# The next image's x asked for in 16 pieces, at the pace of the weight slots

## The reference

```python
g = gn(x)                                # 32 groups of 16 channels
h = relu(bn1(conv1x1(g, conv1_w)))       # 512 -> 128 channels
q = bnq(conv1x1(h, q_w))                 # 4 heads x 16
k = softmax(conv1x1(h, k_w))             # 16
v = bnv(conv1x1(h, v_w))                 # 32
content = einsum(k, v)
pos = conv2d(v, emb)                     # 15 x 15, 16 kernels, for every channel of v
h = q . content + q . pos                # 4 heads x 32 = 128 channels
h = bn3(conv1x1(relu(bn2(h)), conv3_w))  # 128 -> 512
out = x + relu(h + g)
```

## Time and profile before

| | us |
|---|---|
| median of 3 runs (lowest, highest) | 5223.51 (5220.97, 5228.06) |
| the profiled execution | 5228.72 |
| its span in the trace | 5227.0 |
| TensorE busy | 4672.8 |
| VectorE busy | 2957.6 |
| ScalarE busy | 2282.6 |
| mean granted TensorE clock | 0.926 |

### The profile page before, as it was taken

One profiled execution on the slowest core, in us unless ns is written; L12 is line 12 of the kernel. 1 busy time (PEld: TensorE's weight loads), 2 busy tenths in 40 slices (PEclk: granted clock), 3 DMA queues, 4 the chain that ended last, 5 costly groups with the idle time before them and its releaser, 6 DMA issues.

```text
span 5227.0 us, 121426 instructions
## 1 busy us (share of the span) xinstructions
PE 4672.8 (89%) x49366; PEld 2740.0 (52%) x49366; DVE 2957.6 (57%) x4695; ACT 2282.6 (44%) x2816; POOL 748.4 (14%) x433
## 2 busy tenths in 40 slices
PE   4899999899999899999899999999988999999897
PEld 2555555555455555555555555455555555555454
DVE  4465565565555565545656556556556555556553
ACT  1444444444444454444444444444444444445443
POOL 0011110111111111101111111111111111011111
PEclk8898999999999999999989998999999899989998
DMA  3678766678666787666786667876667876678765
GB/s 97 190 237 280 239 212 233 232 251 282 216 213 232 239 271 257 196 227 233 250 278 206 218 229 238 281 243 210 243 225 251 281 233 200 236 234 266 262 192 201
DMA packets 540244, 1217.09 MB, mean 233 GB/s; under 512 B 54312, under 2 KB 236588, under 8 KB 539820
## 3 DMA queue, kind: packets, MB, share of 16 engines
q1 hardware_dynamic: 474348, 950.15, 56.1%
q10 hardware_dynamic: 65472, 260.05, 14.0%
HBM read 777.68 MB, written 365.22 MB: 219 GB/s over the span
## 4 chain that ended last, share of the span: by engine, by line
PE 50%; issue 12%; DVE 12%; DMA 8%; SPq 7%; ACT 7%; POOL 2%; ACTq 0%; DVEq 0%; POOLq 0%
PE ring L498 13%; PE ring L643 13%; PE ring L517 9%; PE ring L573 6%; SPq L387 5%; DMA h<-S 4%; PE ring L597 4%; DMA X<-x_dram 3%; PE ring L524 2%; POOL X L1166 2%; ACT region L782 2%; PE ring L607 2%; DVE S L1010 2%; DVE ring L1014 2%; DVE region L965 2%
## 5 line engine op out<-in xcount | busy, mean ns | idle before, releaser
L691 ACT COPY region<-ring 126x1024 f32<-126x1024 f32 x1184 | 1163.2, 1015 | 1137.4 <-PE ring L498 1127.9
L573 PE MATMUL ring<-h,w3T 128*128 128x512 f32 x2048 | 1016.3, 637 | 130.7 <-DVE S L1010 82.1
L517 PE MATMUL ring<-X,w1e 128*128 128x512 f32 x2048 | 911.0, 598 | 49.7 <-DVE w1e L887 28.9
L498 PE MATMUL ring<-Qt,Ep 96*126 96x256 bf16 x5120 | 851.4, 308 | 101.3 <-ACT region L691 65.7
L643 PE MATMUL ring<-region,V 126*32 126x128 f32 x24576 | 875.2, 287 | 20.4 <-issue 20.4
L498 PEld LDWEIGHTS ring<-Qt,Ep 96*126 96x126 bf16 x5120 | 626.6, 152 | 346.9 <-issue 171.2
L643 PEld LDWEIGHTS ring<-region,V 126*32 126x32 f32 x24576 | 675.0, 115 | 240.6 <-issue 230.1
L691 DVE COPY region<-ring 126x1024 f32<-126x1024 f32 x352 | 430.1, 1222 | 630.7 <-PE ring L498 630.7
L863 DVE BATCH_NORM_STATS2 st<-X 128x6 f32<-128x512 f32 x1024 | 624.6, 677 | 207.2 <-DMA X<-x_dram 207.1
L573 PEld LDWEIGHTS ring<-h,w3T 128*128 128x128 f32 x2048 | 381.2, 199 | 570.2 <-issue 366.9
L517 PEld LDWEIGHTS ring<-X,w1e 128*128 128x128 f32 x2048 | 382.4, 190 | 527.9 <-issue 478.2
(11 more groups left out here) (127 smaller groups left out, 3069.5 us busy)
## 6 DMA issues: line engine op xcount, KB each, us to landing
X<-x_dram SPq DMA_DIRECT2D x132, 2048.0 KB, 21.0
out_dram<-X SPq DMA_DIRECT2D x512, 512.0 KB, 9.9
X<-x_dram ACTq DMA_DIRECT2D x124, 2048.0 KB, 9.4
Qt<-q_parts SPq DMA_DIRECT2D x768, 128.0 KB, 4.1
V<-v_windows SPq DMA_DIRECT2D x96, 1024.0 KB, 8.2
h<-S SPq DMA_DIRECT2D x1024, 64.0 KB, 2.0
q_parts<-region SPq DMA_DIRECT2D x128, 256.0 KB, 3.2
v_windows<-region SPq DMA_DIRECT2D x64, 512.0 KB, 5.8
```

Source lines behind the costliest of these rows:

```text
L498: last = nc.tensor.matmul(dst[0:TROWS, i * 256:(i + 1) * 256], taps(u, xo, yo), Q[:, :, xo * BLK + yo, :], start=(i % 2 == 0), stop=True, ...
L517: last = nc.tensor.matmul(dst[:, hh * HALF:(hh + 1) * HALF], w1e[:, c, :], X[:, j, c, hh * HALF:(hh + 1) * HALF], start=(c == 0), stop=(c ...
L573: last = nc.tensor.matmul(dst[:, yb * HALF:(yb + 1) * HALF], w3T[:, t, :], src, start=True, stop=True)
L691: return engine_copy(dst, src)
```

## The change

Three things are changed, and nothing in what is computed.

1. x of the next image is loaded in 16 pieces of 512 KB, one for each chunk j and channel tile c, each with a semaphore of its own. Piece n is issued after `X_AFTER[n]` slots of units 1 and on have been generated by TensorE (24 for the last one, the end of unit 3's slots); the first piece of a chunk still waits for the stores of the chunk too.
2. `load_v3` is issued behind piece 7 instead of behind all of x.
3. The statistics go piece by piece, two parts for each, and stand at other places among VectorE's slots (`STATS_AT`); `c0` waits for the 16 semaphores.

`x_turn` is only counted up, and nothing waits for it.

```diff
@@ -41,7 +41,11 @@
 ACT_SLOTS = [(u, s) for u in range(UNITS) for s in range(NS) if s not in BY_DVE[u]]
 DVE_SLOTS = [(u, s) for u in range(UNITS) for s in range(NS) if s in BY_DVE[u]]
 
-STATS_AT = {0: (0, 0, 0, 0, 0, 1, 1, 1), 1: (1, 1, 1, 2, 1, 1, 2, 1), 2: (1, 1, 1, 2, 1, 1, 2, 1), 3: (1, 1, 1, 1, 1, 2, 1, 1)}
+STATS_AT = {0: (0, 0, 0, 0, 2, 0, 2, 0), 1: (2, 0, 2, 0, 2, 0, 2, 0), 2: (2, 0, 2, 0, 2, 0, 2, 0), 3: (2, 0, 2, 0, 2, 2, 2, 2)}
+
+
+X_AFTER = [0, 1, 2, 4, 6, 7, 9, 11, 12, 14, 16, 18, 19, 21, 23, 24]
+V3_AFTER = 7
 
 
 VEC_TILES = [0, 2, 3, 5, 7, 8, 10, 12, 13, 15]
@@ -265,8 +269,9 @@
         pool_out = sem("pool_out")
         dve_link = sem("dve_link")
 
-        x_in = [sem(f"x_in{j}") for j in range(NCH)]
+        x_in = [[sem(f"x_in{j}{c}") for c in range(CT)] for j in range(NCH)]
         res_in = [sem(f"res_in{j}") for j in range(NCH)]
+        x_turn = sem("x_turn")
         out_done = [sem(f"out_done{j}") for j in range(NCH)]
         q_out = [sem(f"q_out{j}") for j in range(NCH)]
         q_in = [sem(f"q_in{j}") for j in range(NCH)]
@@ -337,8 +342,8 @@
 
         @block.sync
         def _(sp):
-            def load_x(im, j):
-                sp.dma_start(X[:, j, :, :], xv[im, :, :, j * CHUNK:(j + 1) * CHUNK]).then_inc(x_in[j], 16)
+            def load_x(im, j, c):
+                sp.dma_start(X[:, j, c, :], xv[im, :, c, j * CHUNK:(j + 1) * CHUNK]).then_inc(x_in[j][c], 16)
 
             def reload(b, j):
                 sp.dma_start(X[:, j, :, :], xv[b, :, :, j * CHUNK:(j + 1) * CHUNK]).then_inc(res_in[j], 16)
@@ -396,7 +401,8 @@
 
             for j in range(NCH):
                 sp.sem_inc(out_done[j], HEAD)
-                load_x(0, j)
+                for c in range(CT):
+                    load_x(0, j, c)
             sp.dma_start(w1r, w1).then_inc(setup_in, 16)
             sp.dma_start(w3r, w3.rearrange("(t p) c -> p t c", p=P)).then_inc(setup_in, 16)
             sp.dma_start(wqr, wq).then_inc(setup_in, 16)
@@ -437,8 +443,17 @@
                 if not last:
                     for j in range(NCH):
                         sp.wait_ge(out_done[j], b * (16 * CT) + HEAD)
-                        load_x(b + 1, j)
-                load_v3(b)
+                        sp.sem_inc(x_turn, 1)
+                        for c in range(CT):
+                            n = j * CT + c
+                            if n:
+                                sp.wait_ge(w_full, b * (UNITS * NS) + NS + X_AFTER[n])
+                                sp.sem_inc(x_turn, 1)
+                            load_x(b + 1, j, c)
+                            if n == V3_AFTER:
+                                load_v3(b)
+                else:
+                    load_v3(b)
                 shuffle(b, 0)
                 shuffle(b, 1)
 
@@ -557,7 +572,8 @@
                 elif name == "c0":
                     pe.wait_ge(w1e_ready, im + 1)
                     for i in range(NCH):
-                        pe.wait_ge(x_in[i], im * 16 + 16)
+                        for c in range(CT):
+                            pe.wait_ge(x_in[i][c], im * 16 + 16)
                 elif name == "cl":
                     pe.wait_ge(soft_ready, im * NCH + NCH)
                 elif name == "cp":
@@ -857,9 +873,9 @@
 
             def stats_part(im, n):
 
-                j, hh, c = n // 8, n // 4 % 2, n % 4
-                if n % 8 == 0:
-                    dve.wait_ge(x_in[j], im * 16 + 16)
+                j, c, hh = n // 8, n // 2 % 4, n % 2
+                if hh == 0:
+                    dve.wait_ge(x_in[j][c], im * 16 + 16)
                 return nc.vector.bn_stats(st[:, c, 2 * j + hh, :], X[:, j, c, hh * HALF:(hh + 1) * HALF])
 
             def gn_aggregate(chain, last, im):
```

## The result

The changed kernel takes 5390.23 us (median of 4 runs, 5370.89 to 5401.03) against 5225.78 (4 runs, 5220.97 to 5228.81) of the kernel before: ratio 1.0312, 95% interval 1.0290 to 1.0334. It is 3.1% slower; 5156 was predicted. The profiled execution took 5386.61 us, its span is 5384.9.

A forecast was written before the change was run, and what follows sets the result against it. It took TensorE as the bound, interrupted by late instruction fetches and a lowered clock. The profiled 5228.7 - 81 (first halves) + 11 (c0 waits) + 2 (start) = 5161, with the median 5.2 lower: 5156 us, range 5040 to 5255.

The forecast's parts named there:

- The waits before c0: Before the first c0 product: 12 more semaphore waits cost 0 to 0.7 us per image, taken as 0.35, +11 us.
- V3's term: First half of the lambda stage: V3's load, moved to mid-stretch, delays an instruction fetch by 2.3 us, bounds 0 and 4.3.
- Slower: Rival, chance 0.13: V3 in mid-stretch makes a 4 us hole and the clock falls in every image; 5275 us.
- The first hole: In the first half's rest products (L607): the instruction-fetch hole shrinks from 2.0 us to 1.0, bounds none and as now.
- The clock: First half of the lambda stage: the lower TensorE clock costs 1.2 us instead of 3.7, bounds 0 and 3.7.
- The reading of the bottleneck: First half of the lambda stage: late instruction fetches (3.4 us) and the lowered clock (3.7) lose 7.1 us per image.
- all stalls go: Rival, chance 0.25: with few queued descriptors no fetch is late; first half 30.5 to 31.5 us, total 5032 or 5062.
- That shorter loads would shorten the wait: DMA queues: engines go round rings packet by packet, so shorter loads shorten a fetch's wait; shared the 0.25 chance.
- What was costed at nothing: The piecewise statistics on VectorE, SyncE's 12 more issues and 15 slot waits, and smaller pieces' DMA speed: no cost.

The follow-up runs named there:

- e1: The changed kernel, but c0 waits for 4 of the 16 x semaphores; 5265.19 us, ratio 1.0051.
- e4: The kernel before with 20 semaphore increments added ahead of TensorE's loop, nothing changed inside it; 5342.24 us, ratio 1.0209.
- f4: The changed kernel, all 16 waits kept, with 150 semaphore increments ahead of TensorE's loop; 5290.42 us, ratio 1.0092.
- e2: The changed kernel with V's fourth tile loaded last, behind piece 15, and c0's 16 waits kept; 5241.23 us, ratio 1.0017.
- e3: The changed kernel with V's fourth tile loaded last, behind piece 15, and 4 waits at c0; 5143.63 us, ratio 0.9815.
- g1: f2 with pieces 3 to 7 asked for at slots 5, 8, 9, 10, 12 instead of 4, 6, 7, 9, 11; 5080.67 us, ratio 0.9713.
- f3: e3 without the waits on TensorE's slots, so the 16 pieces go out unpaced once the stores are out; 5223.08 us, ratio 0.9973.
- f2: f1 with V's fourth tile cut into four pairs of transfers, behind pieces 9, 11, 13 and 15; 5099.76 us, ratio 0.9721.
- f1: e3 with V's fourth tile loaded behind piece 11 instead of piece 15; 5144.44 us, ratio 0.9803.
- g2: The kernel before, x in four 2 MB loads, with V's fourth tile in four portions at slots 24 to 30; 5236.81 us, ratio 1.0002.

## Why the prediction was wrong, by its own steps

**The step that failed** is "The waits before c0". The prediction priced them as time between w1e and the first product, "0 to 0.7 us per image", and took 0.35. That price measured 0.65, at the upper bound: 27.05 against 26.39 us, 20 us in the run. In the profile it shows in the row of w1e, 45.4 us for e1's 28.6. (The second half grew by another 0.2 us, to e1's 26.39 from 26.19; every run with the pieces has it, and its cause is open.) But the same instructions also occupy the code of a loop that the prediction itself had read as fetched again in each pass, 13 blocks of 16.4 KB an image, and it didn't ask whether the loop would still touch 13. It touched 14; the sum had this at nothing, without a reason. That cost 30 holes of 5.3 us on average at the loop's top (159.4/30), 113 us net in the mixed stages. The rest of the holes is given back there: TensorE's busy time in the stage is 23 us less (why isn't shown; the granted clock is 0.93 for 0.95), and 24 us lie over waits that were there anyway. e1, e4 and f4 show it from three sides. Without this the change would be e1's: 5265, ratio 1.0051. Of the 158 us lost, the two effects of the waits make 133 (113 + 20).

The traces' records of the DMA packets show what the branch waits for. In each of the 90 branches back to the top in the changed kernel, e2 and e4, exactly one packet of kind instruction starts, 3.4 to 4.0 us after the branch does, and TensorE goes on 1.3 to 1.5 us after it has landed. In the kernel before, e1 and f4 no packet falls into any of the 90 branches. So with 13 blocks the code of the loop's top is on hand when TensorE branches, and with 14 it is fetched while TensorE waits. Where the loop is left it is the other way round in the kernel before: there the code behind the loop is missing (the hole of 4.69 us), and in the changed kernel it is not. The loop is built with a hint for the branch back (`hint_back_edge=True`), an instruction at the loop's top in both; why it suffices in one position and not in the other is not shown. The Trainium skill (Runtime: NRT & Kernel Launch, Instruction fetch mechanics) says that a taken branch whose target isn't in a window of two pages of code has to wait for a fetch of it. The changed kernel's branches of 5.92 us agree; that the same branch of the kernel before, in a loop of 13 blocks, takes 0.36 us isn't explained by it.

The miss in full: the sum had the span 68 us shorter, and it grew by 158. Of these 226 us, 113 are the mixed stages, which the sum didn't touch, 102 the first halves (38.3 us for 35.0), some 15 the second halves (26.5 us for 11), and the rest came out 4 better.

**V3's term was mis-sized.** I took 2.3 us, "near the one hole that V3 made", with an upper bound of 4.3. The holes at L659 are 139.7/31 = 4.5 us an image, up to 7.4. The mechanism was that of the rival "Slower", a hole of 4 us behind V3. Around the hole of the timeline above, SyncE asks for V3 and the DMA engines are full at a low rate. SyncE's issues in the changed kernel:

```profile
2632.19 15.11 SPq L346 DMA_DIRECT2D X<-x_dram  x7
2647.35 0.96 SPq L385 DMA_DIRECT2D V<-v_windows  x2
2648.70 18.50 SPq L346 DMA_DIRECT2D X<-x_dram  x8
```

Busy time by stretches of 4 us in it:

```profile
2646.00:2650.00 4.00, 3.78 (x103) 3.08 (x95) 2.80 (x4) 1.74 (x3) 0.00 (x0) 1.00 0.81 247
2650.00:2654.00 4.00, 3.37 (x101) 2.71 (x102) 3.14 (x6) 3.42 (x4) 0.00 (x0) 1.00 1.03 251
2654.00:2658.00 4.00, 1.65 (x43) 1.32 (x42) 0.14 (x1) 0.25 (x1) 0.00 (x0) 1.00 1.07 195
```

In the last of them the engines are as full as they were behind the stores, at 195 GB/s for 419, and TensorE gets 1.65 us of work done. The prediction read V3's own cost from a window in which only V3 was left, at share 0.72. In the middle of the stretch pieces of x come on top, and the hole is larger on average than with either alone. That V3's place makes it is shown by e2, where it falls to 35.0 us with V3 last. The term took a hole read at a low share for a place with a high one.

**The first hole** was about right: 1.0 us taken, 14.9/31 = 0.5 measured. **The clock** was taken at 1.2 us. Busy time is 32.91 in the first half, over a floor of 30.4, so it costs 2.5; behind the long hole the groups run slow (1.97 us for 1.09 in the timeline above). With these the stretch is 30.4 + 0.5 + 4.5 + 2.5 = 37.9, and 0.4 of waits for copies make the 38.3 that was measured; 35.0 was predicted.

**The reading of the bottleneck was right.** That the holes without a releaser are waits for code was inferred in the prediction. The packets bear it out: of the 539 such holes of 1 us or more in the twelve traces, 535 end 0.5 to 1.95 us (median 1.5) after a packet of kind instruction has landed, of which there are only 13 or 14 in a pass of some 160 us. These holes, and the clock behind them, were where a gain lay: e3 and g1 take the first half to 33.2 and 32.9 us, within 2.7 and 2.4 of the floor of 30.5. The rival "all stalls go" put it at 30.5 to 31.5, and no version got there. That shorter loads would shorten the wait, which the prediction drew from a rule of the Trainium skill, is not borne out by f3: the holes at the rest products are 74.9 us with 512 KB pieces and 71.7 with loads of 2048 KB. The Trainium skill (DMA: Bandwidth & Descriptors, Queues, rings and completion order) has a DMA engine go round its rings packet by packet. By that alone the depth of another ring wouldn't matter; but with the same loads the pace takes these holes from 74.9 us (f3) to 48.7 (e3), so the runs show more than the rule gives.

**What was costed at nothing** held. The statistics follow piece by piece with a wait of 46.2 us, and TensorE's own waits for copies don't show it. SyncE's 12 more issues and its waits on the slots cost nothing: e1, which has them all, has the mixed stages of the kernel before. The small pieces cost nothing that can be seen: f3 is no slower than the kernel before (0.9973).

The rival "Slower" had the right side and the right hole behind V3, at 5275 (its own terms, 45 and 11 to 23, give 5280 or more); it did not have the loop's top. Without the loop's top and the waits the change is still no gain (e1, 1.0051): V3's place costs what the pace gives, for with V3 last the first halves fall from 1200.5 us (e1) to 1027.8 (e3). No case of the prediction, and not the range up to 5255, held 5390.

## What to carry to other kernels

Where the page shows instruction packets in number (blocks times passes) and holes with the releaser "issue", count how many blocks a pass touches before and after any edit to that engine, waits included, and compare the packets on the new page first. The duration of the loop's branch tells the rest: 0.36 us or 5.92 here. One block more cost over five times what the waits themselves took. In this kernel bulk loads beside a long stream of code were better paced than asked for at once (e3 against f3), and the load in short packets was best cut into portions between the others (f2 against e3 and f1). A stall's price that was read in a quiet window was too low for a busy one. And a load moved in a queue moves what stands behind it: x in f1, the shuffle in g2.

## What was unexpected of the hardware

Twenty semaphore increments outside the loop cost 2.1% of the kernel (e4), and 150 took 100 us off another kernel (f4, 5290 for 5390), at 22.3 us of their own, 0.15 us each. A wait of TensorE that has nothing to wait for is not free either: 12 of them took 0.65 us, 0.05 each. In the view of the line's instructions of the changed kernel they are these:

```profile
L576 PEldq EVENT_SEMAPHORE  x225: 51/51/51, 74.7 to 5173.5; - x113
```

The kernel before has 33 there, so 12 more waits are 192/32 = 6 instructions an image, two waits in each. Each is recorded with 51 ns, but in the trace they start 0.106 us apart, and six times that is 0.64 us, the whole price: the recorded duration is half of what such an instruction takes. Open is what in the DMA engines holds a fetch of 16.4 KB back: the traces show that it comes late behind full queues, and latest behind V3's short packets (1 KB, those of x are 4 KB), but not behind which packets it stood.
